# Layer 1 attention of a four-layer decoder: the value projection taken out of the batch loop, and the order of work around it rewritten

## What is computed

```python
xn = layernorm(x, ln_x_g, ln_x_b)
ln = layernorm(latents, ln_l_g, ln_l_b)
q = ln @ W_q
kv = jnp.concatenate([xn @ W_kv, ln @ W_kv], axis=1)
k, v = (kv[..., :INNER], kv[..., INNER:])
q, k, v = (to_heads(q), to_heads(k), to_heads(v))   # 2 heads of 64
qn = rmsnorm(q, q_gamma) * SCALE
kn = rmsnorm(k, k_gamma)
sim = jnp.einsum('bhid,bhjd->bhij', qn, kn)
sim = jnp.where(full_mask[:, None, None, :], sim, neg)
attn = jax.nn.softmax(sim.astype(jnp.float32), axis=-1)
out = jnp.einsum('bhij,bhjd->bhid', attn, v)
return out @ W_out + b_out
```

## Time and profile before

| | |
|---|---|
| runs, median | 2246.82 us |
| runs, lowest and highest | 2244.03, 2247.71 us |
| the profiled execution, own time | 2248.04 us |
| its span, first to last instruction | 2246.3 us |
| PE busy over the span | 94% |
| DVE, ACT, POOL busy over the span | 67%, 54%, 33% |
| mean granted TensorE clock | 0.953 of full speed |

### The profile page before, as it was taken

One profiled execution on the slowest core, in us unless ns is written; L12 is line 12 of the kernel. 1 busy time (PEld: TensorE's weight loads), 2 busy tenths in 40 slices (PEclk: granted clock), 3 DMA queues, 4 the chain that ended last, 5 costly groups with the idle time before them and its releaser, 6 DMA issues. The chain is left out here.

```text
span 2246.3 us, 48142 instructions
## 1 busy us (share of the span) xinstructions
PE 2102.4 (94%) x19158; PEld 1551.7 (69%) x19158; DVE 1497.3 (67%) x3097; ACT 1222.4 (54%) x2377; POOL 749.4 (33%) x305
## 2 busy tenths in 40 slices
PE   6999999768999799999999999999997889999996
PEld 3677777657888545577777777777774457777774
DVE  5777777687878445466666666666635567777784
ACT  5877877535666232354444444444431367777763
POOL 6665664035656193111211112111100163443310
PEclk7999999868999799899999999999997979999998
DMA  6555454213331211112211131112000254444420
GB/s 164 144 144 153 137 146 121 69 41 118 122 120 53 58 38 48 67 59 74 102 60 59 59 109 67 59 59 92 9 1 20 79 150 131 128 149 123 139 78 9
DMA packets 94160, 199.82 MB, mean 89 GB/s; under 512 B 41729, under 2 KB 49969, under 8 KB 93682
## 3 DMA queue, kind: packets, MB, share of 16 engines
q1 hardware_dynamic: 93938, 196.74, 29.3%
HBM read 116.22 MB, written 0.65 MB: 52 GB/s over the span
## 5 line engine op out<-in xcount | busy, mean ns | idle before, releaser
L1619 PEld LDWEIGHTS L2ps<-L2probsT,L2values 125*128 125x128 f32 (+1 forms) x2688 | 317.5, 192 | 51.3 <-issue 49.2
L1600 PE MATMUL L2ps<-L2keys,L2qz 128*128 128x501 f32 x672 | 340.8, 591 | 0.9 <-DVE L2out_bias L1836 0.9
L1619 PE MATMUL L2ps<-L2probsT,L2values 125*128 125x128 f32 (+1 forms) x2688 | 318.4, 275 | 0.5 <-ACT L2probsT L1729 0.5
L1812 DVE CUSTOM_DVE_ANT_0 L2work<-L2ps,L2maskadd,L2big 128x1503 f32<-128x1503 f32 x112 | 199.5, 1781 | 74.3 <-PE L2ps L1600 74.2
L1614 PEld LDWEIGHTS L2ps<-const,L2work 128*126 128x126 f32 x1344 | 164.6, 140 | 118.6 <-issue 116.7
L1714 POOL TENSOR_TENSOR L2keys<-L2keys,L2mean_spread 127x1500 f32<-127x1500 f32 x15 | 51.5, 3432 | 578.6 <-DMA L2wqk<-L_moments 578.6
L654 ACT ACTIVATE L3probsT<-L3ps 128x448 f32<-128x448 f32 x384 | 196.3, 547 | 71.1 <-PE L3ps L511 66.3
L654 ACT ACTIVATE L0probsT<-L0ps 128x448 f32<-128x448 f32 x384 | 198.4, 552 | 47.4 <-PE L0ps L511 46.3
L1614 PE MATMUL L2ps<-const,L2work 128*126 128x128 f32 x1344 | 202.9, 274 | 3.5 <-DVE L2work L1821 3.1
L1731 ACT COPY L2qz<-L2ps 128x128 f32<-128x128 f32 x112 | 29.8, 266 | 304.9 <-PE L2ps L1619 304.9
L798 DVE TENSOR_REDUCE L0partmax<-L0ps 112x1 f32<-112x1000 f32 x128 | 153.4, 1198 | 58.3 <-PE L0ps L484 56.2
(11 more groups left out here) (470 smaller groups left out, 4283.7 us busy)
## 6 DMA issues: line engine op xcount, KB each, us to landing
L0key_stack<-L0key_parts SPq DMA_DIRECT2D x192, 187.5 KB
L3key_stack<-L3key_parts SPq DMA_DIRECT2D x192, 187.5 KB
L0ctxT<-in_ctxT SPq DMA_DIRECT2D x16, 750.0 KB, 4.4
L1raw<-in_ctx SPq DMA_DIRECT2D x16, 750.0 KB
L1rawT<-in_ctxT SPq DMA_DIRECT2D x16, 750.0 KB, 6.2
L2raw<-in_ctx SPq DMA_DIRECT2D x16, 750.0 KB
L3ctxT<-in_ctxT SPq DMA_DIRECT2D x16, 750.0 KB, 4.4
L2mean_spread<-L_moments SPq DMA_DIRECT2D x15, 750.0 KB, 6.8
```

What stands on the lines that cost most here:

```text
L1600: last = nc.tensor.matmul(PS[:, 3 * (m % 2) + c, 0:NPR], tile_rows(m), KT[:, m // RT % 2, 500 * c:500 * c + NPR], start=True, stop=True)
L1619: last = nc.tensor.matmul(PS[:, bank, 0:P], V[0:keys_in(c), i // RT % 2, c, :], PT[0:keys_in(c), i % 2, c, :], start=c == 0, stop=c == NCH ...
L1812: nc.vector.tensor_tensor_reduce(SM[:, m % 2, :].rearrange("p (c n) -> p c n", c=3), PS[:, 3 * (m % 2):3 * (m % 2) + 3, 0:NPR], MA[:, m // ...
```

## The change

- The value projection goes: no V units, no `V` tile. O multiplies `PT` by the raw context `RAW`. The reciprocal deviation `rs`, which scaled `V`, scales the rows of `PT` when T3 is emptied. The centring, the gain, the value weights and `W_out` become one 128 x 128 matrix per head, `WVO[:, 0, h]`; for the token values it is `WVO[:, 1, h]`, and the token rows enter O turned but not projected, in columns of their own. So Z is two transposes, `HT` four times as large, and Y four matmuls (two kinds by two heads) instead of one.
- T3 is emptied by ACT, DVE, ACT, ACT: on ACT one scaling instruction per chunk (eight) and one copy, on DVE one multiplication by the broadcast `rs`. T2 is emptied by ACT alone.
- O of n moves to iteration n + 1, behind K, and Z of n behind T2 there. The scores of n + 1 stand together, each waiting for its own third of `KT`. The last O and Z follow the loop.
- POOL's product into `KN` becomes three instructions, and T2 waits for its third.
- DVE: `stats` is split into `statistics` (of n + 4, before Z) and `aggregate` (of n + 3, behind its share of T3, from n = 1); `stats(3)` is in n = 0; Z comes late in the iteration, `key_sums` last.
- `RAW` has six buffers, each loaded by two DMAs (112 rows and 13 rows); its reload waits for O of six batches before. Batches 2 and 3 are loaded at the start of the attention without a wait.
- Ahead of the loop: two more small products and a transpose, four matmuls for `WVO` and its copy; 16 transposes in place of the 16 matmuls for the token values; the difference `XM` is taken before `stats(0)`.

```diff
-    kv = lambda b, js: [u for j in js for u in (("K", b, j, "D"), ("V", b, j, "A"))]
-    turned_keys = lambda b: [("T2", b, j, "ADA"[j]) for j in range(3)]
+    keys = lambda b: [("K", b, j, "D") for j in range(3)]
+    turned_keys = lambda b: [("T2", b, j, "A") for j in range(3)]
...
-        units += [("T3", n, j, "DAAD"[j]) for j in range(4)]
+            units += keys(n + 2)
+        if n:
+            units += [("O", n - 1, 0, "A")]
+        if n == B // 2 + 1:
+            units += [("Y", 0, 0, "D")]
+        units += [("T3", n, j, "ADAA"[j]) for j in range(4)]
         if n + 1 < B:
             units += turned_keys(n + 1)
...
+        if n:
+            units += [("Z", n - 1, 0, "D")]
...
     def load_raw(self, sp, b):
-        sp.dma_start(self.RAW[:, b % 2], self.src["ctx"][b]).then_inc(self.ctx_loaded[b % 2], 16)
+        for rows in (slice(0, TT), slice(TT, CH)):
+            sp.dma_start(self.RAW[rows, b % 6], self.src["ctx"][b][rows]).then_inc(self.ctx_loaded[b % 6], 16)
...
# PE
-                        nc.tensor.matmul(PS[0:TT, bank, 0:P], PT[:, c, :], V[:, b % 3, c, :], start=c == 0, stop=False)
-                    last = nc.tensor.matmul(PS[0:TT, bank, 0:P], PT[0:Q, NCH, :], VL[:, b, :], start=False, stop=True)
+                        nc.tensor.matmul(PS[0:TT, bank, 0:P], PT[:, c, :], RAW[:, b % 6, c, :], start=c == 0, stop=c == NCH - 1)
+                    last = nc.tensor.matmul(PS[0:TT, bank, P:2 * P], PT[0:Q, NCH, :], VL[:, b, :], start=True, stop=True)
...
-                    last = nc.tensor.matmul(PS[:, bank, 0:HALF], W[:, 3, :], HT[:, b * HALF:(b + 1) * HALF],
-                                            start=True, stop=True)
+                    for n in range(2 * H):
+                        last = nc.tensor.matmul(PS[:, bank, 0:HALF], WVO[:, n // H, n % H, :],
+                                                HT[:, n // H, n % H, b * HALF:(b + 1) * HALF], start=n == 0, stop=n == 2 * H - 1)
...
             def scores(b, parts):
-                    for j in range(1, 3):
-                        wait_emptied(pe, plan.emptied("T2", b, j))
...
+                    wait_emptied(pe, plan.emptied("T2", b, min(c, 2)))
...
                 if n + 2 < B:
                     for j in range(3):
                         unit("K", n + 2, j)
-                        unit("V", n + 2, j)
+                if n:
+                    unit("O", n - 1, 0)
+                if n == B // 2 + 1:
+                    unit("Y", 0, 0)
                 for j in range(4):
                     unit("T3", n, j)
                 if n + 1 < B:
                     for j in range(3):
                         unit("T2", n + 1, j)
-                unit("O", n, 0)
...
+                if n:
+                    unit("Z", n - 1, 0)
                 if n + 1 < B:
-                    scores(n + 1, range(2))
-                unit("Z", n, 0)
-                if n + 1 < B:
-                    scores(n + 1, range(2, 4))
+                    scores(n + 1, range(4))
+            unit("O", B - 1, 0)
+            unit("Z", B - 1, 0)
...
# POOL
-                nc.gpsimd.tensor_tensor(by_head(KN[:]), by_head(K[:, b % 2]), rk[:].unsqueeze(2).to_broadcast([CH, 24, HD]),
-                                        ALU.mult).then_inc(s.k_normed, 1)
+                for j in range(3):
+                    nc.gpsimd.tensor_tensor(by_head(KN[:, 4 * j:4 * j + 4]), by_head(K[:, b % 2, 4 * j:4 * j + 4]),
+                                            rk[:, 8 * j:8 * j + 8].unsqueeze(2).to_broadcast([CH, 8, HD]), ALU.mult).then_inc(s.k_normed, 1)
...
# ACT
-                    ins = nc.scalar.copy(PT[:, 4 * j:4 * j + 4, :].rearrange("p c n -> p (c n)"), PS[0:CH, bank, 0:4 * TT])
+                    act.wait_ge(s.rs_ready, b + 1)
+                    for c in range(4 * j, min(4 * j + 4, NCH)):
+                        ins = nc.scalar.mul(PT[:, c, :], PS[0:CH, bank, (c % 4) * TT:(c % 4 + 1) * TT], rs[:, b, c:c + 1])
+                    if j == 3:
+                        ins = nc.scalar.copy(PT[0:Q, NCH, :], PS[0:Q, bank, 0:TT])
...
             for n in range(B):
-                if n + 2 < B:
-                    empty("V", n + 2, 0)
                 if n:
                     exp(n)
-                if n + 2 < B:
-                    empty("V", n + 2, 1)
-                    empty("V", n + 2, 2)
-                empty("T3", n, 1)
-                empty("T3", n, 2)
+                if n:
+                    empty("O", n - 1, 0)
+                for j in (0, 2, 3):
+                    empty("T3", n, j)
+                if n + 1 < B:
+                    for j in range(3):
+                        empty("T2", n + 1, j)
                 if n + 2 < B:
                     squares(n + 2)
-                if n + 1 < B:
-                    empty("T2", n + 1, 0)
-                    empty("T2", n + 1, 2)
-                empty("O", n, 0)
-                if n + 2 < B:
                     mask(n + 2)
...
# DVE
-                    if j < 3:
-                        ins = nc.vector.tensor_copy(PT[:, 4 * j:4 * j + 4, :].rearrange("p c n -> p (c n)"), PS[0:CH, bank, 0:4 * TT])
...
+                    ins = nc.vector.tensor_tensor(PT[:, 4 * j:4 * j + 4, :],
+                                                  PS[0:CH, bank, 0:4 * TT].rearrange("p (c n) -> p c n", c=4),
+                                                  rs[:, b, 4 * j:4 * j + 4].unsqueeze(2).to_broadcast([CH, 4, TT]), ALU.mult)
...
                 if n:
                     maximum(n)
-                    empty("Z", n - 1, 0)
...
-                empty("T3", n, 0)
-                empty("T3", n, 3)
+                if n == B // 2 + 1:
+                    empty("Y", 0, 0)
+                empty("T3", n, 1)
+                if 1 <= n and n + 3 < B:
+                    aggregate(n + 3)
...
+                if n == 0:
+                    stats(3)
+                if n + 4 < B:
+                    statistics(n + 4)
+                if n:
+                    empty("Z", n - 1, 0)
                 if n + 2 < B:
                     key_sums(n + 2)
-                for b in ([3, 4] if n == 0 else [n + 4]):
-                    if b < B:
-                        stats(b)
```

More of the change, by code:

```diff
@@ L990, in _ @@
         def _(sp):
[L991 to L993 removed]
+            ahead.load_raw(sp, 2)
+            ahead.load_raw(sp, 3)
             for b in range(2, B):
[L995 removed]
+                sp.wait_ge(s.filled, plan.filled("K", b - 2, 2))
                 ahead.load_turned(sp, b)
@@ L1008, in unit @@
                     wait_emptied(pe, plan.before(what, b, j))
-                if what in "KV":
+                if what == "K":
                     pe.wait_ge(ctxt_loaded[b % 2], 16 * (b // 2 + 1))
-                    if b == 0 and j == 1 and what == "V":
-                        pe.wait_ge(s.bias_ready, 1)
+                    if b == 0 and j == 1:
+                        pe.wait_ge(s.products_ready, 1)
                     for i in range(4):
-                        last = nc.tensor.matmul(PS[0:CH, bank, i * P:(i + 1) * P], chunk(b, 4 * j + i), WF[:, "KV".index(what), :],
+                        last = nc.tensor.matmul(PS[0:CH, bank, i * P:(i + 1) * P], chunk(b, 4 * j + i), WF[:],
                                                 start=True, stop=True)
                 elif what == "T2":
-                    pe.wait_ge(s.k_normed, b + 1)
+                    pe.wait_ge(s.k_normed, 3 * b + j + 1)
                     for i in range(4):
@@ L1058, in _ @@
             pe.wait_ge(s.fold_in, 1)
[L1059 to L1064 removed]
+            nc.tensor.matmul(PS[:, 7, 0:P], CEN[:], GW[:, 0], start=True, stop=True)
+            nc.tensor.matmul(PS[0:CH, 7, P:2 * P], BB[:], W[:, 1, :], start=True, stop=True)
+            nc.tensor.matmul(PS[:, 5, 2 * P:2 * P + 1], W[:, 2, :], k.v("L1_xb"), start=True, stop=True)
+            nc.tensor.matmul(PS[:, 7, 2 * P:3 * P], GW[:, 1], CEN[:], start=True, stop=True)
+            last = nc.tensor.transpose(PS[:, 7, 3 * P:4 * P], W[:, 2, :], k.ident)
+            last.then_inc(s.folded, 1)
+            ln_turn(pe, k, s, PS)
+            pe.wait_ge(s.turned_ready, 1)
+            for x, values in enumerate((GV, VT)):
+                for h in range(H):
+                    rows = slice(h * HD, (h + 1) * HD)
+                    last = nc.tensor.matmul(PS[:, 5 + h, x * P:(x + 1) * P], values[rows], W[rows, 3, :], start=True, stop=True)
+            last.then_inc(s.products, 1)
+            nc.tensor.matmul(PS[:, 5, 2 * P + 1:2 * P + 2], W[:, 3, :], BV[:], start=True, stop=True).then_inc(s.bias_filled, 1)
             pe.wait_ge(s.ln_done, 2)
@@ L1072, in _ @@
                 unit("K", 0, j)
-                unit("V", 0, j)
-            pe.wait_ge(s.xm_ready, 1)
             pe.wait_ge(s.qk_copied, 1)
             pe.wait_ge(s.kk_copied, 1)
+            pe.wait_ge(s.xm_ready, 1)
             for b in range(B):
-                last = nc.tensor.matmul(PS[0:Q, b // 4, (b % 4) * P:(b % 4 + 1) * P],
```

(22 more changed lines are left out.)

102 lines of the change are left out of this document (42 added, 60 removed).

## The result

| | before | after |
|---|---|---|
| median of 3 runs | 2246.82 us | 2212.03 us (2208.43 to 2212.04) |
| ratio, 95% interval | | 0.9843 (0.982 to 0.9865) |
| the profiled execution, own time | 2248.04 us | 2212.03 us |
| its span | 2246.3 us | 2210.2 us |
| mean granted TensorE clock | 0.953 | 0.953 |

The kernel is 1.6% faster, and a ratio of 1 lies outside the interval. But the attention itself gained 41.7 us, and the whole span only 36.1. Of the 5.6 us between them 1.0 stands ahead of the attention, whose start moved from 472.2 to 473.2 us, and 4.6 behind it. They are the part of the result that the prediction didn't have, and one question of the experiments.

What follows compares the result with a forecast made beforehand. TensorE was taken to bound the attention loop; -11.5 (preparation, iterations 0 and 1), -23.0 (iterations 2 to 13), -2.5 (Y) and -3 (tail) gave -40.0 us, from 2248.04 to 2208.0, median 2207 us; range 2196 to 2222.

Steps and rivals of the forecast that it cites:

- The loop PE - ACT - PE at 12.3 us: Attention iteration: ACT's emptying of T3 and T2 follows the removed V; 12.3 us for 14.22, PE idle some 0.7 us.
- M + 11.9: Attention iteration: length of the loop over POOL, with M the start of DVE's maximum, taken as 1.5 us.
- ACT's scalings at 0.26 us: Emptying of T3: ACT's eight scalings start 0.26 us apart, four taking 1.1 us; the skill's rule gave 0.39 each.
- POOL's thirds "just in time": POOL's product in three parts, ready at 6.8, 7.8 and 8.8 us against T2 at 7.65, 8.1 and 8.65.
- Preparation and iterations 0 and 1, -11.5 us: Attention's start to its third pass: PE starts that pass at 548.5 for 560.0, -11.5 us, between -7 and -14.
- Iterations 2 to 13, -23.0, and Y, -2.5 us: Attention loop: twelve times 14.22 - 12.3, -23.0 us; Y in the middle 3.0 us without a stall, -2.5 us.
- Tail, -3 us: Attention's end: O fills two PE stalls of 3.69 us, Y 2.3 us longer; 27.5 for 30.5 us, +0.5 to -4.5.
- Later stages begin behind a barrier and don't move.: Stages behind the layer 1 attention: no change in their time.
- (1): Rival, attention loop: PE and DVE full, iteration 11.7 us, 7 us better, 2199 to 2200 us; chance 0.21.
- (2): Rival, attention loop: Z, scalings or POOL's thirds cost more, iteration 13.3 us, 2221 us; chance 0.21.
- (3): Rival, attention loop: the chain key_sums, power, product, T2, scores keeps 14.2 us; only preparation, Y, tail gain; 2230 us; chance 0.04.
- (4): Rival, attention loop: brief PE idling lowers its clock, 4.9 us per iteration, 69 us in all, 2276 us; chance 0.04.

Runs made afterwards that it cites:

- v_work_back: Kernel after, with each K unit's four matmuls issued twice, giving TensorE its old amount of work: 2247.91 us, iteration 14.66 us for 12.15.
- act_late: Kernel after, with a useless 448-column copy on ACT between T3 and T2 in iterations 2 to 13: 2217.55 us, iteration 12.51 us for 12.15.
- act_early: Kernel after, with a useless 448-column copy on ACT ahead of the exponential in iterations 2 to 13: 2203.14 us, iteration 12.15 us, unchanged.
- scores_all: Kernel after, with the first scores waiting for the last third of KT instead of the first: 2228.18 us, iteration 12.98 us for 12.15.
- shared_more: Kernel after, with T3 emptied by DVE, ACT, DVE, ACT, Z's copies on ACT, stats(2) before the first maximum: 2207.49 us, iteration 12.18 us.
- kn_one: Kernel after, with POOL's product into KN in one instruction instead of three: 2216.15 us, iteration 12.85 us for 12.15.
- again: Kernel after, run once more with no edit: 2209.87 us, ratio 0.9839.
- sums_early: Kernel after, with key_sums back in its old place on DVE, ahead of statistics and Z: 2238.70 us, iteration 14.39 us for 12.15.
- dve_ballast: Kernel after, with two useless 448-column products on DVE behind the reciprocal in iterations 2 to 13: 2221.06 us, iteration 13.09 us for 12.15.
- raw_one: Kernel after, with a batch's raw rows loaded by one DMA of 125 rows, not 112 and 13: 2209.50 us, iteration 12.15 us.

## Why the prediction was right, step by step

- **TensorE bounds the loop, and V is 2.73 us of it.** Shown by v_work_back, 2.51 us of 2.73 back.
- **The loop PE - ACT - PE at 12.3 us.** Up to the first scores every event came within 0.25 us of its place; behind them ACT's last copy of T2 ended 0.3 us early, its squares 0.4, and the next maximum came 0.4 early. Work of ACT behind T3 lengthens the loop, and work ahead of the exponential doesn't: act_late, act_early and scores_all show it. Two things about the loop were wrong. PE's idle time was to stand in three places, 0.7 us, ended by ACT in front of T2 and in front of the scores. It was 0.3 us an iteration, 3.9 in twelve: ACT ends the wait in front of T2, but nothing is waited for in front of the scores, and T2's last unit follows POOL, which was to be the sign of another loop. And the loop over POOL, "M + 11.9", was 12.17 (shared_more), so that the two nearly tie at 12.15 and neither alone can be shortened. DVE's 11.6 us were 11.16; I had added the start-to-start times of rows of which some held short gaps.
- **ACT's scalings at 0.26 us.** From 591.49 to 593.39 they started 0.24 us apart. The Trainium skill, "ScalarE: Activation LUTs", Rules for kernel authors, has about 0.3 us for each plus 0.83 ns per element, 0.39 us; as a price of one ACTIVATE alone that agrees with the trace, where each took 0.34 to 0.40 us, but a row of them overlaps, and the sum of 1 us more did not come.
- **POOL's thirds "just in time".** Right that the product had to be cut: kn_one lost 0.70 us per iteration. The last third is late by a little in nearly every iteration, as the profile after shows; the prediction's own times, 8.8 us for the third and 8.65 for T2, had it so.
- **SP's waits cost nothing.** Right. The load on the DMA engines rose to 112 GB/s, as worked out.
- **Preparation and iterations 0 and 1, -11.5 us.** Measured -12.6: 75.2 us from the block's start to the third pass for 87.8 (in the profile of again 73.6). The parts were less good. The first maximum came 2.5 us earlier within the block, not 0.5, the second 9.1 and not 7.3. Up to 1.55 us of that is a power on POOL that took 3.84 us in the profile before and 2.29 in the 13 others, the one with the old order too. So it doesn't come from the change; without it this part would be some -11.
- **Iterations 2 to 13, -23.0, and Y, -2.5 us.** Measured -24.6 for twelve times 2.05 or 2.08 and -2.5 for Y: the iteration with Y is 2.9 us longer, before it was 5.4 with the stall behind it.
- **Tail, -3 us.** Measured -2.0, 30.3 us for 32.3, where the prediction counted 27.5 for 30.5: the block ends at 768.5 us, at the next stage's first transposes, and not at 767. O fills PE's wait for the exponential, but T3 still waited 1.75 us and T2 for POOL's second and third part (0.38 us each), which the count left out. In return the clock stayed up, 1.00 for 0.78.
- **"Later stages begin behind a barrier and don't move."** This step failed. They took 4.6 us longer: 5.1 more in the layer 2 attention, by the clock at its start, which goes either way from one execution to the next, and 0.5 less in the others. Two profiles can differ by 7 us for that alone. The medians may carry some of it, 2212.03 and 2209.87 us for the same kernel, but runs without a profile don't show their stages. The forecast of -40.0 us was met by -41.7 in the attention and -34.8 in the medians.
- **The rivals.** (1), PE and DVE full at 11.7, was kept off by the loop over POOL. (2), 13.3 us, did not come. (3) is what sums_early made. (4) did not come: with some 0.3 us of idle time in each iteration, no gap above 0.31 us, the clock was 1.00 for 149 us. That is half of the 0.7 us that the prediction gave PE, but sums_early covers it: over five of its iterations, 569.84 to 641.79 us, PE idled 10.6 of 71.95 us, in one gap of 1.47 us and three of 0.2 us each time, and the clock was 1.00 as well. The Trainium skill, "TensorE: Matmul & The Clock Gate", section A second HAM failure mode, describes a kernel whose clock swings under brief idling between groups; here it did not.

## What to carry to other kernels

Work taken from a full engine is worth only what the next loops leave: here 2.73 us came off TensorE, and the old order would have passed on 0.77 of it. Before such a change, add up each engine and each closed chain of waits per iteration, and place what waits longest (here `key_sums`, behind the squares) last in its engine's order. And before a few microseconds in a distant stage are explained, look whether that stage starts behind idle time, and take a second profile of the same kernel.

## What the runs showed of the hardware

**DVE and POOL in each other's way.** In dve_ballast the two products on DVE are alike, 448 columns from two SBUF operands. The first one of an iteration, begun under POOL's product, took 1.45 us in nine of twelve iterations; all the others took 0.60 to 0.63 (duration in ns, least, median, most; then the stretch itself):

```profile
L1386 DVE TENSOR_TENSOR L1ballast<-xnT x24: 601/628/1454, 557.1 to 701.7; 128x448 f32<-128x448 f32 x24
```

```profile
608.49 1.04 POOL L1151 TENSOR_TENSOR L1kn<-L1keys,L1rk 125x512 f32<-125x512 f32 x1
608.56 2.00 DVE L1386 TENSOR_TENSOR L1ballast<-xnT 128x448 f32<-128x448 f32 x2
609.49 2.65 POOL L1140 TENSOR_TENSOR L1rs<-L1ve,half_neg 125x12 f32<-125x12 f32 x1
```

It began as POOL's product did and ended 0.5 us after it, as if it had waited for that product and then run; the power that followed on POOL took 2.65 us for its usual 2.27. The change's own DVE work shows none of this: its product into `PT`, with an operand in PSUM, took 0.62 us beside the same POOL product.

**A load of 125 rows slows its neighbours.** In raw_one the load of `CT`, issued right behind that of the raw rows, landed later than in the kernel after (groups of DMAs from 560 to 700 us, raw_one and then after; the last number is the median time to landing):

```profile
L1rawT<-in_ctxT SPq DMA_DIRECT2D x9, 750.0 KB, 11.6
```

```profile
L1rawT<-in_ctxT SPq DMA_DIRECT2D x9, 750.0 KB, 6.5
```

The same bytes took 11.6 us behind one load of 125 rows and 6.5 behind loads of 112 and 13. It takes a load right behind: the kernel before had the one load of 125 rows too, but issued `CT` 5.3 us after it, and `CT` landed in 5.7 us (median, 560 to 736 us). Here 18 us of cover hide it. The Trainium skill, "DMA: Bandwidth & Descriptors", How many engines, says that a load is spread over the largest number of DMA engines, up to 16, that divides the slowest dimension of both its sides. If that dimension is the rows here, it is 5 engines for 125 rows and 16 for 112. The two landings agree with that; the engines themselves weren't read.
